# Index words of the expert stage: another queue, packed row numbers, a later index

## The reference, cut to what matters

```
logits = xt @ Wg.T + bg
top_vals, top_idx = top_k(logits, 2);  rw = softmax(top_vals)
gu = xt @ Wgu[e] + bgu[e];  gate = min(gu[..., ::2], 7);  up = clip(gu[..., 1::2], -7, 7)
gated = (up + 1) * gate * sigmoid(1.702 * gate)
out_e = gated @ Wd[e] + bd[e];  out = sum of rw * out_e over the token's two experts
```

## Time and profile before

| | |
|---|---|
| timed, median of 3 | 670.28 us |
| profiled execution, span from first to last instruction | 699.0 us |
| PE busy in the span | 551.6 us (79%) |
| DVE busy | 479.4 us (69%) |
| ACT busy | 328.5 us (47%) |
| POOL busy | 345.7 us (49%) |
| mean granted TensorE clock | 0.913 |

### The profile page before, as it was taken

One profiled execution on the slowest core, in us unless ns is written; L12 is line 12 of the kernel. 1 busy time (PEld: TensorE's weight loads), 2 busy tenths in 40 slices (PEclk: granted clock), 3 DMA queues, 4 the chain that ended last, 5 costly groups with the idle time before them and its releaser, 6 DMA issues.

```text
span 699.0 us, 12908 instructions
## 1 busy us (share of the span) xinstructions
PE 551.6 (79%) x3216; PEld 294.1 (42%) x3217; DVE 479.4 (69%) x1334; ACT 328.5 (47%) x707; POOL 345.7 (49%) x455
## 2 busy tenths in 40 slices
PE   1896979778878788888879599978588999999910
PEld 0575534322434434334433245544244555555500
DVE  4577545857568685849675648868575777777796
ACT  3862753464687666656755133422232333333331
POOL 4757440442865866676774513445532333333353
PEclk9999988759999998979997779999999999999955
DMA  9912000039101010100010112355553333333398
GB/s 312 297 41 24 0 5 0 1 110 302 46 3 34 32 47 21 41 21 34 29 54 8 62 31 68 86 91 136 149 148 77 90 82 70 82 88 91 99 377 295
DMA packets 93415, 62.61 MB, mean 90 GB/s; under 512 B 68338, under 2 KB 78710, under 8 KB 93240
## 3 DMA queue, kind: packets, MB, share of 16 engines
q1 hardware_dynamic: 85352, 44.12, 23.5%
q0 software_dynamic: 6864, 16.86, 7.1%
q10 hardware_dynamic: 1152, 1.06, 0.5%
HBM read 27.97 MB, written 25.56 MB: 77 GB/s over the span
## 4 chain that ended last, share of the span: by engine, by line
PE 32%; DVE 21%; SPq 15%; issue 13%; ACT 8%; another core or an unknown queue 4%; DMA 4%; POOL 3%; ACTq 0%; DVEq 0%; POOLq 0%
SPq L416 8%; PE bank L1154 7%; PE bank L968 4%; SPq L417 3%; PE bank L1170 3%; SPq L412 3%; DVE AR L1559 2%; PE bank L957 2%; ACT AR L803 2%; DVE X L1880 2%; DVE MX L1547 2%; PE bank L995 2%; PE bank L1015 2%; DMA X<-in_x 2%
## 5 line engine op out<-in xcount | busy, mean ns | idle before, releaser
L665 POOL DMA_INDIRECT y_rows<-AR,CST x79 | 77.2, 977 | 152.3 <-ACT AR L903 142.1
L892 ACT ACTIVATE AR<-AR 128x256 f32<-128x256 f32 x79 | 32.9, 417 | 148.8 <-DVE AR L1788 120.1
L543 POOL TENSOR_TENSOR W<-STG,W 128x512 f16<-128x512 f32 (+1 forms) x48 | 55.5, 1162 | 55.5 <-ACT W L706 53.5
L622 POOL DMA_INDIRECT xs_rows<-AR,SLOT x64 | 63.3, 988 | 36.6 <-issue 19.5
L1559 DVE RECIPROCAL AR<-bank 128x512 f32<-128x512 f32 x16 | 53.7, 3355 | 25.7 <-PE bank L1154 25.3
L803 ACT ACTIVATE AR<-bank 104x1024 f32<-104x1024 f32 (+1 forms) x48 | 48.4, 1022 | 46.1 <-PE bank L1138 23.0
L1547 DVE TENSOR_REDUCE MX<-bank 128x8 f32<-128x616 f32 x64 | 48.5, 794 | 27.5 <-PE bank L1103 14.8
L1804 DVE TENSOR_TENSOR AR<-bank,AR 128x256 f16<-128x256 f32 x79 | 33.6, 425 | 34.8 <-ACT AR L896 31.8
L1788 DVE TENSOR_SCALAR AR<-bank 128x256 f32<-128x256 f32 x79 | 33.3, 422 | 29.9 <-PE bank L1295 24.3
L1154 PE MATMUL bank<-AR,VCUR 104*32 104x512 f32 (+1 forms) x256 | 40.9, 744 | 13.8 <-issue 10.0
L1302 PE MATMUL bank<-ID,AR 128*128 128x128 f32 x158 | 33.0, 291 | 21.6 <-DVE AR L1799 15.9
(11 more groups left out here) (249 smaller groups left out, 1413.9 us busy)
## 6 DMA issues: line engine op xcount, KB each, us to landing
W<-in_wexp SPq DMA_DIRECT2D x16, 768.0 KB, 5.6
W<-y_rows SPq DMA_DIRECT2D x8, 1024.0 KB, 14.7
X<-in_x SPq DMA_DIRECT2D x4, 1024.0 KB, 12.7
out<-X SPq DMA_DIRECT2D x8, 512.0 KB, 8.6
CST<-in_cst SPq DMA_DIRECT2D x1, 1309.0 KB, 9.1
CST<-xs_rows SPq DMA_DIRECT2D x79, 1.0 KB
y_rows<-AR,CST POOLq DMA_INDIRECT x79
xs_rows<-STG SPq DMA_DIRECT2D x9, 129.0 KB
```

Source lines behind the costliest of these rows:

```text
L543: pool.tensor_tensor(w[:, 1], STG[:, q], w[:, 0], ALU.subtract).then_inc(s["w_split"], 1)
L622: pool.indirect_dma_start(xs_rows, bass.IndirectOffsetOnAxis(ap=SLOT[:, par, k, j:j + 1], axis=0), RB[:, par, j, :], None, bounds_check=XS ...
L665: pool.indirect_dma_start(y_rows, bass.IndirectOffsetOnAxis(ap=NIX[:, k:k + 1], axis=0), CY[:, k, :], None, bounds_check=TOPK * NTOK - 1, ...
```

## The change

It has three parts. The index words are loaded by ACT (`meta`) two slots ahead, behind `c_y` of slot n-2, and no longer by SP; with them the wait on `nix_r` leaves SP. The row numbers of two neighbouring slots are packed in one word of a new table ROW2 (the odd one's block number times 1024 plus the even one's), so that SP and ACT each load one word for two slots and take it apart (`row_pair`); DVE makes ROW2 with two more small operations in `copies`. In the loop of DVE, and in the written-out slots behind it, `c_index` stands behind `c_glu` instead of behind `c_gate`; in the first 32 slots it stood there already. ACT gets the waits ahead of its first load and, in slot 30, the waits for the padding that SP has at the same point.

```diff
+RADIX = 1024
+LASTROW = NEXP * CAP // P
+        def row_pair(eng, t):
+            v = eng.value_load(ROW2[0:1, ds(t, 1)], min_val=0, max_val=LASTROW * (RADIX + 1))
+            return [nc.s_assert_within(r, 0, LASTROW) * P for r in (v % RADIX, v // RADIX)]
...
-            def load(n, q, first=False):
-                row = sp.value_load(TAB[0:1, ds(P + n, 1)], min_val=0, max_val=XS_ROWS - P)
+            def load(n, q, row, first=False):
                 if not first:
                     sp.wait_ge(s["cgu_mm"], n - (IN - 1))
-                    sp.wait_ge(s["nix_r"], n - (IN - 1))
                 sp.dma_start_transpose(XTS[q], xs_halves[ds(row, P), 0:2 * D]).then_inc(XTIN[q], 16)
-                sp.dma_start(META[:, q, :], xs_rows[ds(row, P), D:ROW]).then_inc(RINS[q], 16)
...
             with sp.Fori(EARLY // IN, NSLOT // IN) as t:
-                for q in range(IN):
-                    load(t * IN + q, q)
+                for q in range(0, IN, 2):
+                    rows = row_pair(sp, t * 2 + q // 2)
+                    load(t * IN + q, q, rows[0])
+                    load(t * IN + q + 1, q + 1, rows[1])
...
+            def meta(q, row):
+
+                act.dma_start(META[:, q, :], xs_rows[ds(row, P), D:ROW]).then_inc(RINS[q], 16)
+
+            for q in range(2):
+                act.wait_ge(SCT[q], 16 * TOPK * GT * EARLY_GROUPS // 2)
+            act.wait_ge(s["c_cp"], 2)
+            rows = row_pair(act, 0)
+            meta(0, rows[0])
+            meta(1, rows[1])
+            rows = row_pair(act, 1)
             c_tanh(0, 0)
+            meta(2, rows[0])
             c_tanh(1, 1)
             c_gh(0, 0)
+            meta(3, rows[1])
             for n in range(2, EARLY):
                 c_tanh(n, n % 2)
                 c_gh(n - 1, (n - 1) % 2)
                 c_y(n - 2, (n - 2) % IN, (n - 2) // IN)
+                if n == EARLY - 2:
+                    act.wait_ge(s["pads0"], 16 * (NEXP // 2 + 1))
+                    act.wait_ge(s["pads1"], 16 * (NEXP // 2))
...
+                if n % 2 == 0:
+                    rows = row_pair(act, (n + 2) // 2)
+                meta((n + 2) % IN, rows[n % 2])
...
                     c_tanh(t * IN + k, k % 2)
                     c_gh(t * IN + (k - 1), (k - 1) % 2)
                     c_y(t * IN + (k - 2), (k - 2) % IN, t if k >= 2 else t - 1)
+                    if k % 2 == 0:
+                        rows = row_pair(act, t * 2 + k // 2 + 1)
+                    meta((k + 2) % IN, rows[k % 2])
...
+                dve.tensor_scalar(ROWF[0:1, n0:n1], rows[:, P + n0:P + n1], 1.0 / P, None, ALU.mult)
...
+                two = ROWF[0:1, :].rearrange("p (t v) -> p t v", v=2)
+                dve.scalar_tensor_tensor(out=ROW2[0:1, a0:a1], in0=two[:, a0:a1, 1], scalar=float(RADIX),
+                                         in1=two[:, a0:a1, 0], op0=ALU.mult, op1=ALU.add)
...
                 for k in range(IN):
                     c_gate(t * IN + k, k % 2)
-                    c_index(t * IN + k, k, t)
                     c_gl(t * IN + (k - 1), (k - 1) % 2)
                     c_glu(t * IN + k, k % 2)
+                    c_index(t * IN + k, k, t)
```

More of the change, by code:

```diff
@@ L214, in build_decoder @@
         CWI = free(578 + 13 * NEXP, NEXP, I32)
+        ROWF = free(594 + 13 * NEXP, P)
+        ROW2 = free(594 + 13 * NEXP + P, P // 2, I32)
         w_flat = W16[:, :, :, :].rearrange("p n v w -> p (n v w)")
@@ L409, in _ @@
             xs_halves = xs_rows.bitcast(F16)
-            def load(n, q, first=False):
-                row = sp.value_load(TAB[0:1, ds(P + n, 1)], min_val=0, max_val=XS_ROWS - P)
+            def load(n, q, row, first=False):
                 if not first:
                     sp.wait_ge(s["cgu_mm"], n - (IN - 1))
-                    sp.wait_ge(s["nix_r"], n - (IN - 1))
                 sp.dma_start_transpose(XTS[q], xs_halves[ds(row, P), 0:2 * D]).then_inc(XTIN[q], 16)
-                sp.dma_start(META[:, q, :], xs_rows[ds(row, P), D:ROW]).then_inc(RINS[q], 16)
             for n in range(EARLY):
-                load(n, n % IN, n < IN)
+                if n % 2 == 0:
+                    rows = row_pair(sp, n // 2)
+                load(n, n % IN, rows[n % 2], n < IN)
                 if n == EARLY - NEXP // 2 - 1:
@@ L432, in _ @@
             with sp.Fori(EARLY // IN, NSLOT // IN) as t:
-                for q in range(IN):
-                    load(t * IN + q, q)
+                for q in range(0, IN, 2):
+                    rows = row_pair(sp, t * 2 + q // 2)
+                    load(t * IN + q, q, rows[0])
+                    load(t * IN + q + 1, q + 1, rows[1])
             for n in range(NSLOT // IN * IN, NSLOT):
-                load(n, n % IN)
+                if n % 2 == 0:
+                    rows = row_pair(sp, n // 2)
+                load(n, n % IN, rows[n % 2])
             full = sp.value_load(REAL[0:1, 0:1], min_val=TOPK * NTOK // P, max_val=NSLOT)
@@ L911, in _ @@
                 c_y(n - 2, (n - 2) % IN, (n - 2) // IN)
+                if n == EARLY - 2:
+                    act.wait_ge(s["pads0"], 16 * (NEXP // 2 + 1))
+                    act.wait_ge(s["pads1"], 16 * (NEXP // 2))
+                    for q in range(2):
+                        act.wait_ge(SCT[q], 16 * TOPK * TILES // 2)
+                    act.wait_ge(s["c_cp"], 4)
+                if n % 2 == 0:
+                    rows = row_pair(act, (n + 2) // 2)
+                meta((n + 2) % IN, rows[n % 2])
                 if n == 5:
@@ L938, in _ @@
                 c_y(n - 2, (n - 2) % IN, (n - 2) // IN)
+                if n + 2 < NSLOT:
+                    meta((n + 2) % IN, row_pair(act, (n + 2) // 2)[0])
             c_gh(NSLOT - 1, (NSLOT - 1) % 2)
@@ L1865, in _ @@
                     c_gate(t * IN + k, k % 2)
-                    c_index(t * IN + k, k, t)
                     c_gl(t * IN + (k - 1), (k - 1) % 2)
                     c_glu(t * IN + k, k % 2)
+                    c_index(t * IN + k, k, t)
             for n in range(NSLOT // IN * IN, NSLOT):
                 c_gate(n, n % 2)
-                c_index(n, n % IN, n // IN)
                 c_gl(n - 1, (n - 1) % 2)
                 c_glu(n, n % 2)
+                c_index(n, n % IN, n // IN)
             c_gl(NSLOT - 1, (NSLOT - 1) % 2)
```

## The result

The changed kernel takes 666.75 us, the median of 10 executions (664.51 to 668.35), against 670.55 us (669.28 to 673.99, 10 executions) for the kernel before on the same chip. The ratio is 0.9939, with a 95% interval of 0.992 to 0.9957. It is faster by 0.6%, which is 4.1 us where 8.2 were forecast.

The account below looks back on a forecast made before the run. SP's issuing was taken to bound the expert stage. Loop 5.4 plus padding 4.5, less ACT 1.0 and table operations 0.3, gave 8.6 us, scaled to 8.2: 662.0 us, range 655.5 to 670.0.

Parts of the forecast that it names:

- What bounds the kernel: Expert stage: SP's queue, full with issuing at 2.87 us a slot; behind it a DVE, ACT and PE circle at 2.70.
- 32 x (2.87 - 2.70) = 5.4 us: Loop and tail: 32 slots at SP's pace of 2.87 us fall to the other engines' 2.70, gaining 5.4 us.
- Padding, 4.5 us, and ACT's cost, 1.0 us: First 32 slots: PE's waits for slots 30 and 31 and slow clock go, 4.5 us; ACT's added work loses 1.0.
- ACT has cover in the loop: Loop: ACT's long block of 1.2 to 1.4 us fits its idle time ahead of tanh, costing nothing.
- The wait on `nix_r` off SP: no price, no gain: Expert stage: the circle waits for nothing there, so removing SP's wait has no price and no gain of its own.
- Index behind the gated value: 0: DVE in the loop: the later index may cost 0.1 us every second slot; taken as 0, bound 2.8 us.
- Each instruction is likely dearer when profiled: Whole kernel: timed median 28.7 us below the profiled span, so the 8.6 us gain was scaled by 0.959 to 8.2.
- rival 3: Only the loop's gain comes, as DVE and ACT bind the padding stretch: about 666.4 us, chance 0.10.
- Rival 1: No change, 670.3 us: timed executions lack SP's issue gaps, so SP's pace is already below 2.70 us; chance 0.12.
- the Trainium skill's sentence: Issuing DMAs from several engines saves only sequencer time, usually small beside the transfer; by it time stays at 670.3 us.
- Rival 2: Slower: ACT's issue of index words outlasts its cover; at 1.1 us an issue, 676.8 us; chance 0.13.
- rival 4: More than forecast: pace in the loop falls to 2.49 us, 9 us more gain, 653 us; chance 0.07.

Follow-up runs that it names:

- experiment 3: Kernel before with only the row numbers packed two to a word; index words on SP, index behind the gate: 669.68 us, ratio 0.996.
- experiment 6: Kernel before with packed row numbers and the index behind the gated value; index words stay on SP: 664.1 us, ratio 0.9915.
- experiment 9: Kernel before with packed row numbers, index behind the gated value and all final sums on DVE; index words on SP: 663.34 us, ratio 0.987.
- experiment 10: Kernel before with packed row numbers and all final sums on DVE; index words on SP, index behind the gate: 664.86 us, ratio 0.992.
- experiment 2: Changed kernel with the index back behind the gate: 670.93 us, ratio 1.0019 to the kernel before.
- experiment 11: Changed kernel with the index back behind the gate and all final sums on DVE: 663.76 us, ratio 0.989 to the kernel before.
- experiment 8: Changed kernel with all final sums on DVE, run again in a later session: 662.13 us, ratio 0.9861 to the kernel before.
- experiment 1: Changed kernel with DVE waiting for the last scatter to land before the final sums: 671.61 us, ratio 1.003 to the kernel before.
- experiment 4: Changed kernel with all final sums on DVE, ACT's and POOL's share removed: 660.43 us, ratio 0.9867 to the kernel before.
- experiment 7: Changed kernel with the read back held until PE has done slot 78's first product: 664.19 us, ratio 0.9921 to the kernel before.
- experiment 5: Kernel before with all final sums on DVE, ACT's and POOL's share removed: 670.04 us, ratio 1.0005.

## Why the prediction was right and wrong, point by point

- **What bounds the kernel.** Right. In the second trace of the kernel before the last 32 slots run at 2.85 us and in the changed one at 2.71, and SPq is gone from the chain. The 46 slots from slot 32 on take 124.7 us, where about 124 were forecast. The views of the earlier trace rows did say it, though the trace was of a disturbed execution.
- **32 x (2.87 - 2.70) = 5.4 us.** Measured 4.3, since the undisturbed pace of SP is 2.85 and the other engines' is 2.71.
- **Padding, 4.5 us, and ACT's cost, 1.0 us.** Net 3.5 forecast, 4.35 measured. Slots 31 and 32 came 5.53 and 4.14 us behind the one before, and now 2.62 and 2.65, which is 4.4 us and the whole of it; the clock of the stretch goes from 0.98 to 1.00. No cost of ACT's extra work is seen: the first 32 slots take 104.7 to 105.9 us in the kernels with the words on SP (experiments 3, 6, 9, 10) and 104.3 to 104.6 with them on ACT. What the move to ACT buys lies here and in slots 32 to 46, 0.6 to 1.8 us in the two together. That the two terms add up to the forecast 8.6 us is luck in part: the loop brought 1.1 us less than forecast, the first 32 slots 0.85 us more.
- **ACT has cover in the loop.** Right. Its idle time ahead of tanh falls from 1.71 us (80.3 / 47) to 1.55, as the row from 497 to 622 us shows, all of it ended by DVE; the issue takes 0.34 us:

```profile
L903 ACT ACTIVATE AR<-AR 128x256 f32<-128x256 f32 x47 | 19.6, 417 | 72.8 <-DVE AR L1830 72.8
```

```profile
571.57 0.34 ACTq L918 DMA_DIRECT2D CST<-xs_rows  x1
```

- **"The wait on `nix_r` off SP: no price, no gain".** Right from slot 32 on: SP keeps it in experiment 6 and the pace there is the same. In the first 32 slots of the kernel before SP did wait for the index, 12 times and 8.6 us in all; whether that is a part of the gain of those slots was not tried. In the changed kernel SP waits for PE, which is what the prediction wanted to see:

```profile
SPq L422 <- PE bank L1333: 59.0, 48, 2.9
```

- **"Index behind the gated value: 0".** Wrong by sign and size. I looked for what the later place costs (0.1 us of DVE) and not for what the wait of the index holds up in the front place. The price is 2.7 us in experiment 2 and 3.2 us in 11 against 8. Against the kernel before it is no gain of that size, since in its second trace the index waits for no landing at all. Experiment 2 has the first of these rows, the changed kernel the second:

```profile
DVE CST L1855 <- DMA y_rows<-AR,CST: 4.1, 3, 2.8
```

```profile
DVE CST L1855 <- DMA y_rows<-AR,CST: 1.6, 2, 1.2
```

  So the late place keeps what packing wins from being lost to landings that come late, most of them beside the early read back. The second row is also one of the prediction's own signs of being wrong ("if DVE's index waits for a transfer"): it came true in slots 76 and 78, through the landing of a scatter and not of index words, and it points at the same early read back.
- **The sizes of the parts.** By the prediction's own numbers packing alone takes SP to 2.87 - 0.34 + 0.08 = 2.61 us, below 2.70. The move of the index words was then not needed for the loop. It did not draw that conclusion, and experiments 3, 6, 9 and 10 did.
- **The sum was right, the end was not in it.** This is the step that failed: 8.6 us "off the span" took it that the last slot's gain reaches the end. The stage gave 8.6 us (4.35 + 4.27) and the tail took 3.3 back, the start of the stage 0.8, which lies within the spread of the traces (every profiled execution but the first one and that of experiment 8 reaches it between 391.3 and 393.9 us). The prediction asked what bounds the loop once SP is faster, and not what else then comes early: an SP that is no longer late issues eight transfers of 1 MB 14.4 us sooner, DVE finds its data there, and POOL's last scatter and POOL's own sums stand until DVE's unbroken sums are done. Experiments 1, 4 and 7 each take this away in another way; 4 and 7 get time back, 1 pays more than it gets.
- **"Each instruction is likely dearer when profiled", x 0.959.** Wrong premise. The profiled execution was disturbed for 30 us, mostly ahead of the stage. The scaling moved the sum by 0.4 us only.
- **Rivals.** None of the five cases is what happened; the time (666.75 us) lies in the forecast's own range and is the size of rival 3, but its mechanism, one gain only, is false: both gains came. Rival 1, and the Trainium skill's sentence beside it, fell with the pace of 2.71 us: time in SP's queue was worth about 4 us in 32 slots. Nearly all of it came from packing, and what that sentence is about, issuing from a second engine, brought 0.6 to 1.8 us with the move to ACT. Rival 2 fell with ACT's 0.34 us, and rival 4 with the same 2.71.

How the tail locks: for 16.72 and 23.05 us a scatter stood on POOL whose instruction takes 0.97 us in the loop, under unbroken VectorE instructions with two inputs in SBUF (W and X). The second trace of the kernel before and those of the changed kernel and of experiments 2, 4, 5, 6 and 8 to 11 agree on when it ends: 0.85 us after the first pause or the end of VectorE's sums, however long the scatter has stood by then (2.46 to 23.05 us). The Trainium skill (SBUF — State Buffer, "SBUF: two separate sides") has the rule that would have pointed there: VectorE and GpSimd share a pair of ports as an exclusive lock, which a VectorE instruction with two SBUF inputs takes against a GpSimd operation that reads SBUF, and a box there tells that GpSimd's own DMAs then can't get their descriptors written, though it names only VectorE's two-port modes for it. The traces agree in what is seen, with two things left over: the scatter stood across some 40 VectorE instructions, and the scatter of slot 77, 1.4 us earlier and beside the same sums, took only 1.11 us. That it is the lock is argued from the page; what the runs show is that the stretching goes when the scatter comes first (experiment 1), ends early when VectorE pauses (the kernel before, 6) and lasts to the end of the sums when it doesn't (4 and 5).

## What to carry to other kernels

Taking an engine's queue off the bound moves everything it issues later, too: follow that queue to the program's end and ask what its earlier transfers meet there. Order the waits of an in-order engine by who is behind them: a wait that is almost always satisfied should stand behind the work that others want, not ahead of it. And profile the kernel before twice when its span lies per cents above its timed median; and when a bound falls by several edits, work out the pace after each one alone: the smallest that passes the next bound is nearly enough (here packing).

## What the hardware showed that I had not expected

- A GpSimd scatter of 0.97 us stands for 16.72 and 23.05 us beside back-to-back VectorE sums of 128x256 f32 with two SBUF inputs, and ends 0.85 us after their first pause. A pause of 0.16 us is enough (experiment 6).
- Side by side, both pay: VectorE's chunk takes 2.37 us alone and 3.3 us beside GpSimd, and a GpSimd sum 0.68 us alone (10.91 / 16) and 0.83 us beside VectorE. Two engines bring eight chunks in 26.5 us; VectorE with all the sums does it in about 25.4 us (3.17 us a chunk). The second engine was worth nothing here: in the kernel before, taking it out left the time the same (ratio 1.0005).
- The landing of a scatter took 6.13 us with the read back under way. In the second trace of the kernel before, where the read back is not yet issued, the scatter of the same slot, 72, had landed at the latest 3.9 us after it began (622.23 to 626.10, when the index of slot 76 ran without a wait). From the chain of the changed kernel:

```profile
614.93 6.13 DMA y_rows<-AR,CST
```

- One profiled execution can carry 30 us that the timed ones don't have. Here more waits on the queues of ACT (30.5 us against 2.6) and PE are a part of it; VectorE and GpSimd show no more of them, and the order and the bound are the same.
